# A two-block transformer kernel: every second bias tile made by the scalar engine, where it was every fourth

## The reference, cut to what matters

```python
scores = jnp.einsum('bhqd,bhkd->bhqk', q, k) / np.sqrt(hd)
scores = scores - torus_dist[:, None, :, :] * torus_scale[None, :, None, None]
attn = jax.nn.softmax(scores, axis=-1)
out = jnp.einsum('bhqk,bhkd->bhqd', attn, v)
x = x + out @ Wout
x = x + (gelu(layer_norm(x) @ W1 + b1) @ W2 + b2)
```

## Time and profile before

| | before |
|---|---|
| median of 3 runs | 1373.43 us (1373.4, 1373.43, 1377.46) |
| the profiled execution's own time | 1377.58 us |
| its span, first to last instruction | 1375.7 us |
| PE, PEld busy | 94%, 72% |
| DVE, ACT, POOL busy | 58%, 54%, 55% |
| mean granted PE clock | 0.982 of full |

### The profile page before, as it was taken

The page is one execution under the profiler, slowest core; times in us unless marked ns, Lnnn a source line. Parts: engine busy times, 40 slices in busy tenths (PEclk is TensorE's granted clock), DMA queues, the critical chain, the costliest instruction groups (busy, mean ns, idle before and its releaser), DMA issues. The chain is left out here.

```text
span 1375.7 us, 24533 instructions
## 1 busy us (share of the span) xinstructions
PE 1287.0 (94%) x8789; PEld 995.1 (72%) x8789; DVE 796.0 (58%) x2240; ACT 744.4 (54%) x1246; POOL 754.5 (55%) x939
## 2 busy tenths in 40 slices
PE   4799999999999999999999998899999999999878
PEld 3567778778778778778778776767677676766656
DVE  3766845845845845845844843556656566564552
ACT  3466674674674674674674673454444444444431
POOL 3688876876876876866866864101224032240323
PEclk9899999999999999999999999899999999999888
DMA  8533231331331331331331340726243352434100
GB/s 257 145 96 91 63 116 41 77 116 39 79 116 37 80 117 35 81 117 33 80 121 30 94 132 28 225 72 201 76 155 126 115 169 77 154 108 118 47 2 31
DMA packets 98259, 133.98 MB, mean 97 GB/s; under 512 B 16802, under 2 KB 51498, under 8 KB 98130
## 3 DMA queue, kind: packets, MB, share of 16 engines
q1 hardware_dynamic: 96850, 131.80, 32.5%
q10 hardware_dynamic: 1280, 0.53, 0.2%
HBM read 72.64 MB, written 58.75 MB: 96 GB/s over the span
## 5 line engine op out<-in xcount | busy, mean ns | idle before, releaser
L1406 DVE CUSTOM_DVE_ANT_0 shifted<-score,bias 128x512 f32<-128x512 f32 x512 | 332.1, 686 | 281.1 <-PE score L873 202.5
L633 POOL TENSOR_SCALAR shifted<-shifted,row_max 128x512 f32<-128x512 f32 x512 | 362.3, 720 | 171.3 <-DVE row_max L1406 168.4
L1117 ACT ACTIVATE probs<-turned 128x512 f32<-128x512 f32 x512 | 277.6, 595 | 218.8 <-PE turned L885 218.6
L885 PE MATMUL turned<-ident,shifted 128*128 128x128 f32 x2048 | 269.6, 274 | 4.4 <-ACT probs L1117 4.3
L885 PEld LDWEIGHTS turned<-ident,shifted 128*128 128x128 f32 x2048 | 232.8, 141 | 56.3 <-issue 32.7
L801 PE MATMUL dense<-w_down,hidden 128*128 128x256 f32 x1024 | 261.8, 382 | 2.4 <-ACT hidden L1098 2.4
L626 POOL TENSOR_SCALAR bias<-dist,scale 128x1024 f32<-128x1024 f32 x192 | 214.5, 1118 | 13.5 <-DMA down_bias<-in_L_cond_b 13.5
L873 PE MATMUL score<-k_rows,q_rows 97*128 97x512 f32 x512 | 202.2, 456 | 14.1 <-DMA k_rows<-mask_neg 5.2
L801 PEld LDWEIGHTS dense<-w_down,hidden 128*128 128x128 f32 x1024 | 178.1, 190 | 36.9 <-issue 9.6
L781 PE MATMUL dense<-feat_m,w_up 128*128 128x512 f32 x768 | 192.9, 403 | 9.4 <-DVE feat_m L1363 9.4
L781 PEld LDWEIGHTS dense<-feat_m,w_up 128*128 128x128 f32 x768 | 144.5, 193 | 42.4 <-issue 11.7
(11 more groups left out here) (138 smaller groups left out, 1472.0 us busy)
## 6 DMA issues: line engine op xcount, KB each, us to landing
qk_rows<-qk_high SPq DMA_DIRECT2D x128, 256.0 KB
q_rows<-qk_rows SPq DMA_DIRECT2D x64, 384.0 KB
qk_rows<-qk_low SPq DMA_DIRECT2D x64, 256.0 KB
k_rows<-qk_rows SPq DMA_DIRECT2D x68, 192.0 KB
x_in_t<-in_x SPq DMA_DIRECT2D x8, 512.0 KB, 4.8
x_res<-in_x SPq DMA_DIRECT2D x8, 512.0 KB, 5.6
x_mid<-x_norm SPq DMA_DIRECT2D x8, 512.0 KB, 3.3
x_in_t<-x_mid SPq DMA_DIRECT2D x8, 512.0 KB, 4.1
```

What stands on the lines that cost most here:

```text
L633: ins = pool.tensor_scalar(shifted[:, u % 3, i, :], shifted[:, u % 3, i, :], -1.0, row_max[:, t % 6:t % 6 + 1], ALU.mult, ALU.add)
L885: mm = pe.transpose(turned_bank[z % 2][:, HALF * kk + P * i:HALF * kk + P * i + P], shifted[:, u % 3, i, P * kt:P * kt + P], ident[:, :])
L1117: act.activation(probs[:, u % RING, 2 * pair:2 * pair + 2, :], turned_bank[z % 2][:, :].rearrange("p (a c) -> p a c", a=2), ACT.Exp)\
L1406: dve.tensor_tensor_reduce(shifted[:, u % 3, i, :], score_bank[t % 2], bias[:, u % 2, i, :], 1.0, 3.0e38, ALU.add, ALU.min, row_max[:, t % ...
```

## The change

The rule that picks ACT for a unit goes from `u % 4 == 3` to `u % 2 == 1`: of a turn's 32 bias tiles 16 are made by ACT and 16 by POOL. ACT thus makes units 5, 9, ..., 29 in addition, at its steps 3, 7, ..., 27, and unit 1: that of turn 0 ahead of its first step, those of turns 1 to 7 at step 33 of the turn before. The counts that DVE and POOL wait for follow from a helper that counts the tiles made so far by one engine. Arithmetic, buffers and the order of all other instructions are unchanged.

```diff
-    def bias_by_act(u):
-        return u % 4 == 3
+    def bias_by_act(n, u):
+        return u % 2 == 1
+
+    def biases(n, u, act):
+
+        return sum(bias_by_act(m, v) == act for m in range(n + 1) for v in range(UNITS if m < n else u + 1))
...
                 if n < B:
                     make_bias(n, 0)
-                    make_bias(n, 1)
+                    if not bias_by_act(n, 1):
+                        make_bias(n, 1)
...
-                        if k + 2 < UNITS and not bias_by_act(k + 2):
+                        if k + 2 < UNITS and not bias_by_act(n, k + 2):
                             make_bias(n, k + 2)
...
+                if n == 0 and bias_by_act(0, 1):
+                    make_bias(0, 1)
                 for k in range(STEPS):
...
-                    if n < B and k + 2 < UNITS and bias_by_act(k + 2):
+                    if n < B and k + 2 < UNITS and bias_by_act(n, k + 2):
                         make_bias(n, k + 2)
+                    if n + 1 < B and k == 33:
+                        make_bias(n + 1, 1)
...
-                        if bias_by_act(u):
-                            dve.wait_ge(s["act_bias_ready"], 8 * n + u // 4 + 1)
+                        if bias_by_act(n, u):
+                            dve.wait_ge(s["act_bias_ready"], biases(n, u, True))
                         else:
-                            dve.wait_ge(s["bias_ready"], 24 * n + u + 1 - (u + 1) // 4)
+                            dve.wait_ge(s["bias_ready"], biases(n, u, False))
```

More of the change, by code:

```diff
@@ L749, in turn @@
                         if k == 18:
-                            pool.wait_ge(s["bias_ready"], 24 * n + k + 3 - (k + 3) // 4)
+                            pool.wait_ge(s["bias_ready"], biases(n, k + 2, False))
                             mask(n + 1)
```

## The result

| | before | changed |
|---|---|---|
| median | 1373.97 us of 4 | 1399.46 us of 4 (1394.43 to 1401.4) |
| ratio, 95% interval | | 1.017 [1.0153, 1.0187] |
| profiled execution, its span | 1377.58, 1375.7 us | 1394.43, 1392.6 us |
| mean granted PE clock | 0.982 | 0.986 |

The changed kernel is slower by 1.7%, which is 23 us, against the forecast of 20.

What follows compares the result with a forecast made beforehand. PE was taken to set a turn's length, with 1.3 us idle. Turns 1 to 7 lose 15.3 us, turn 0 5.4, POOL's relief gives 1: 19.7, rounded to 20, on 1373.4 gives 1393.5 us; range 1379 to 1405 us.

Steps and rivals of the forecast that it cites:

- Step 15: Turns 1 to 7: PE already waits 0.60 us for ACT's exponentials, no slack, so the full 1.03 us is lost.
- Step 19: Turns 1 to 7: head_out ends late for its reader on PE, which loses 0.53 us.
- Steps 3, 11, 23, 27: Turns 1 to 7: ACT's results still come 0.1 to 0.3 us before their readers; cost 0.
- Step 7: Turns 1 to 7: feat_a comes late, DVE's subtraction starts 0.63 us later, and PE is 0.63 us late.
- Turn 0: No MLP work to put between: 1.1 us at each of steps 15, 19, 23, 27 and 1.0 at step 7; 5.4 us.
- POOL's relief: Fewer waits for POOL's tiles: gain taken as 1 us, bounds 0 and 3, most waits being hidden.
- PE's share: PE's busy share in turns 1 to 7 falls from 98.7% to about 96.5%, a turn growing to 105.7 us.
- The range: 1379 us, with half of step 15's and step 7's losses absorbed, to 1405 us, a little above the first rival.
- Thin margins: Rival, chance 0.17: steps 3, 11, 23, 27 each cost 0.3 us, 8 us more in all; 1402 us.
- POOL's absence shortens DVE: Rival, chance 0.09: DVE's two-input instructions and normalization shorten, some 0.7 us a turn, 5 us; 1388 us.
- All hidden: Rival, chance 0.09: delayed exponentials and head_out find PE with other work; time stays at 1373 us.
- Faster: Rival, chance 0.06: POOL's queue, not PE, paces the turns; up to half of 14.5 us comes back, 1366 us.

Runs made afterwards that it cites:

- the kernel with those five alone: Of the added tiles only those of units 1, 5, 13, 25 and 29 go to ACT, in all turns; one execution, 1376.94 us.
- ACT loaded alone: Kernel before with all its tiles, plus two unread ACT copies where the change puts its tile, at steps 3, 7, ..., 27; 1.0148, 1395.45 us.
- POOL relieved alone: Kernel before, but POOL leaves out the tiles of units 5, 9, ..., 29 and nobody makes them; ratio 0.9988, 1373.66 us.
- moved, and not in turn 0: Changed kernel with turn 0 as before and, in turns 1 to 7, tiles of units 9, 17, 21 elsewhere on ACT; 1.0002, 1375.72 us.

## Why the prediction was right

It forecast slower by 20 us, of which 2.19 a turn at three named places and 5.4 in turn 0. The places and the mechanism held; two terms were mis-sized and one was missing. That the sum came out within a microsecond of what the places add up to (19.7 against 20.5) is in part luck: step 7 was too small by 2.7 us and the relief of POOL by 1.6, with opposite signs.

- **Step 15**, 1.03 us: 1.04. Right, by the turning's start. Not by its wait, which I had said would grow to 1.6: it is split over `to_tokens` (0.64) and the turning (0.34).
- **Step 19**, 0.53 us: 0.49, and 0.01 once the tile stands behind `head_out`. Right.
- **Steps 3, 11, 23, 27** in turns 1 to 7, and unit 1: 0. Right; the kernel with those five alone shows 0.0 a turn.
- **Step 7**, 0.63 us: 1.01. The step that failed is "starts 0.63 us later" taken as the whole price. DVE's subtraction did start that much later (260.89 - 254.49 = 6.40, 0.67 more than the 5.73 ahead), but it then took 1.10 us in place of 0.74, since more of a POOL instruction lay ahead of it: 0.56 us, where before it was 0.20 (253.58 + 1.11 - 254.49). With ACT loaded alone it took 0.79 us, behind 0.25 us of POOL's, and the place cost 0.68. I had also passed over the exponentials of unit 7 as "the smaller delay": they hold PE for 0.58 us at step 10 (6.31 - 5.73) and DVE adds the rest, 0.43 us, at step 11. The 0.6 us to spare was read from the end of the exponentials (254.57) to the turning (255.18); but PE needed 0.15 us from such an end to its start in the changed kernel (261.34 to 261.49), so only 0.46 was slack. Over seven turns the term was too small by 2.7 us.
- **Turn 0**, 5.4 us: 5.3. The sum is right, its parts nearly: 1.06, 0.96, 1.06 and 1.07 for steps 15, 19, 23 and 27, where I had 1.1 each, and 0.76 at step 7 with 0.5 more at step 8, where DVE's normalization lies beside it, for 1.0. The kernel with POOL relieved alone has 0.46 at step 8 too, so that part comes from POOL's missing tile and was in no term.
- **POOL's relief**, -1: -2.6 us when taken alone, inside the bounds of 0 and 3. I had called the waits for POOL's tiles hidden; the one of 1.14 us in turn 1 wasn't.
- **PE's share** in turns 1 to 7: 97.4%, not 96.5, although a turn grew to 106.0 us, more than the 105.7 forecast. I had kept PE's busy time per turn and divided by the longer turn. But over one turn (204.65 to 308.12 us before, 209.95 to 315.95 changed) PE is busy for 102.36 and 103.48 us with the same 802 matmuls at a granted clock of 1.00. It grows by 0.2 to 0.3 us at each of steps 10, 11 and 21 and by 0.5 ahead of step 18, the places where the turn is longer; elsewhere it stays within 0.1. So of the 2.5 us a turn some 1.4 show as idle time and 1.1 as busy time; the profile models the ends of matmuls, and what PE does in those 1.1 us it doesn't show.
- **The range.** Its lower end of 1379 us was explained by half of the losses of steps 15 and 7, but that is (1.03 + 0.63) / 2 x 7 = 5.8 us, which gives 1388. The 1379 has no working.
- **Not in it**: the stretches at half clock, 1.6 us each.

The sum by what was measured: (1.01 + 1.04 + 0.49) x 7 + 5.3 - 2.6 = 20.5 us, and the block's 22.5 less one stretch is 20.9. With one stretch the block explains 22.5 of the 23 to 25 us between the medians. Where the rest lies is open: a second stretch in some executions, or the part behind the block, which took from 519 to 524 us in the traces.

The rivals. **Thin margins** priced the change at 1402 us, nearer to the measured 1399.46 than my 1393.5, and yet it is wrong: in turns 2 to 6 its four places add nothing, at most 0.04 us that is given back two steps on. The total could not have told the two apart; the starts by place do. **POOL's absence shortens DVE** has something for it in turn 1, where the normalization is 0.8 us shorter. At step 7 of the other turns the subtraction got longer, 1.10 us for 0.74; in turn 0 it got shorter, 1.10 for 1.38. **All hidden** holds for other places: moved, and not in turn 0, the tiles cost 1.0002. **Faster** falls with the relieved kernel: even at no cost to ACT, POOL's relief is worth 0.9988 [0.9975, 1.0002].

## What to carry to other kernels

Work moved to an engine with over a third of its time free (ACT before, in turns 1 to 7) can still cost the bounding engine 1 us for an instruction of 1.15: its price is the delay of the next instruction on that engine for which the bounding one waits, less that instruction's slack. Here the same 56 tiles of turns 1 to 7 cost 17 us in one order (22.5 - 5.3) and 0.3 us in another. So lay the timeline of one turn beside the queue of the receiving engine, find what stands directly behind the new instruction, and put it behind what the bound engine waits for rather than ahead. To find where the time went, subtract starts of one recurring instruction between the two traces; waits are renamed and split, starts aren't.

## What the runs showed of the hardware

- **DVE and POOL hold each other up by order.** In the kernel before, DVE's subtraction of two 128x512 tiles began at 254.49, when POOL's bias tile had 0.20 us left, and ahead of two POOL instructions at 254.67: it took 0.74 us, and they took 1.80 together. In the changed kernel POOL's two began first (260.08) and took 1.37; DVE's began when 0.56 us of the second was left, and took 1.10:

```profile
254.67 1.80 POOL L633 TENSOR_SCALAR shifted<-shifted,row_max 128x512 f32<-128x512 f32 x2
```

  The other cases fit: 0.79 us with 0.25 left (ACT loaded alone), and 1.38 with 0.84 left in turn 0 of before, beside a bias tile that began at 67.91; with no POOL instruction beside it, 0.69 (the first, at 20.08). So in each case DVE's instruction ended some 0.54 us behind the POOL instruction that it had met. The Trainium skill, "SBUF — State Buffer", section "Who interferes with whom", says that a DVE instruction with two SBUF inputs contends with a GpSimd (POOL) instruction that reads SBUF, and that the order of issue decides which of them is held up. These rows agree with both. It makes a change of 0.7 us in timing cost 0.3 us more or less on the critical engine.
- **A wait can cost more than its length.** Where PE's waits at step 15 are longer, each of five traces has one or two stretches in seven turns of 3.4 us at the 1.2 GHz level, with 1.6 us of loss each; six traces without them have none in the block. In which turn differs from run to run, and this kernel was nearly 98% busy on PE.
- **An ACT copy from SBUF of 128x512 took 0.723 us and of 128x256 0.506**, where `probs` and `head_out`, which read PSUM, took 0.595 (median) and 0.38 to 0.39 us for the same shapes. My estimate of the loading experiment was made from those, and was too low. The copies also take their scale from a 128x1 tile, which the other two don't; no run tells which of the two differences makes the 0.12 us.
